# A graph layer with a routed feed-forward: a node group's step run whole after its own edges, and a shorter last group

## The chip, the cores and the metric

The kernel runs on one NeuronCore of one Trainium2 chip. The metric is device time in microseconds (us); lower is better. The engines are named as in the profile: PE (TensorE, matmuls; PEld its weight loads), DVE (VectorE), ACT (ScalarE), POOL (GpSimd), SP (SyncE, which here only issues DMAs).

## The reference

Twelve thousand five hundred nodes of 256 features go through a graph layer and a feed-forward layer that is routed to one of eight experts. Both are added to their input.

```python
# x (12500, 256); src, dst, edge_weight (212500,), dst sorted
msgs = _layernorm(x)[src] * edge_weight[:, None]
agg = segment_sum(msgs, dst, 12500)
x = x + agg @ W.T + b                          # W (256, 256)
xf = _layernorm(x)
H = gelu(xf @ W1 + b1)                         # W1 (256, 1024)
probs = softmax(H @ Wg + bg)                   # Wg (1024, 8)
e = argmax(probs)
x = x + probs[e] * (H @ Wd[e] + bd[e])         # Wd (8, 1024, 256)
```

## The kernel before

**Stages.** First the rows of `x` are normalized and written to a table in DRAM. Then comes the edge stage, which is most of the time: 212,500 edges in 1664 tiles of 128, sixteen tiles to a gather step (104 steps). Then the routed stage: 105 tiles of 128 nodes, sorted by expert, each gathered from `row_table`, multiplied with its expert's weights and scattered to the output.

**Edge stage, gather steps.** POOL issues one indirect DMA for each tile (L402), in order, into a ring of three sections of sixteen tiles. Ahead of every eighth tile it waits until PE has used up the tile that held the place (`s_edge_mm`, L401), so POOL can be at most 48 tiles ahead of PE. For a step PE multiplies the sixteen tiles with narrow one-hot weights into `psR` (L514; this is what frees the section), DVE copies the result to `parts` (L896), PE places the parts into the node columns (L523), and DVE adds them to the running sums `agg` (L886) and prepares the next step's weights (L843, L853).

**Edge stage, group steps.** Edges are sorted by destination, so after four or five gather steps all edges of a group of 512 nodes (four blocks of 128) are in. There are 25 groups (`NF`). A table of 129 steps, `steps_i`, worked out on the chip, tells PE and DVE at every turn of their loops whether a gather step or a group step is next. POOL reads no table and only gathers. A group step, f being the group whose edges are in, does two groups' work:

- for f, `take_sums` on DVE (L920: copy the sums out, clear them), `messages` on PE (L560: multiply with the graph weights), `normalize` on DVE (L993: residual, layer norm), `transpose_xn2` on PE (L570), and the copy `copy_xn2T` on ACT (L457);
- for f - 1, `rank_list` (PE), `hidden` on PE and ACT (the first feed-forward layer, eight chunks of two matmuls, a Gelu after each; then the gate matmul and 32 transposes), `rank_choices` and `add_to_lists` on DVE (they enter the choices of f - 2 into the expert lists), and `second_part` on DVE (copy the hidden rows out, choose the expert).

`messages` of f stands between the third and fourth chunk of `hidden` of f - 1. The first group's step is only its first half (kind `SECTIONS + 1`), and after the loop `hidden` of group 24 runs by itself. SP stores the two parts of the rows (`store_x2`, `store_rows`) and loads the next `x` in the same shifted order; the weights of the eight experts (8 MB) are loaded when the last sums are taken, behind `store_rows` of group 23 on SP. Group 24 holds 212 nodes, but all four blocks are computed and stored.

**End of the edge stage.** The last choices are entered in the lists, DVE builds the order of the nodes (up to L1089), and POOL begins the routed gathers (L416, L419).

Of the kernel before, what the change touches and what calls it, by code (L numbers as in the profile page):

```python
# [15 lines left out]
F32 = mybir.dt.float32  # L16
# [7 lines left out]
P = 128  # L24
N = 12500
# [11 lines left out]
NB = NODES // P  # L37
EDGES = 212500
# [30 lines left out]
PAD_ROW = N + (-N) % 64  # L69
# [23 lines left out]
def build(nc, x, srcT, dstT, wT, gnn_WT, gnn_b, W1, b1T, Wg, bg, Wd, bd, out):  # L93
    assert PAD_ROW + P <= NODES and NB % LN_ROWS == 0
    ctx = ExitStack()
    with ctx:
# [10 lines left out]
        row_dram = nc.dram_tensor("row_table", (NODES, ROW), F32, kind="Internal").ap()  # L107
# [28 lines left out]
        steps_i = sb("steps_i", [P, STEPS, 6], I32)  # L136
# [184 lines left out]
        def _(sp):  # L321
# [25 lines left out]
            def store_x2(f):  # L347

                sp.wait_ge(s_xn2, f + 1)
                sp.dma_start(row_dram[bass.ds(f * GROUP, GROUP), 0:C].rearrange("(q p) c -> p q c", p=P),  # L350
                             xg[:, :, :]).then_inc(s_x2_st, 16)
                sp.wait_ge(s_x2_st, f * 16 + 16)

            def load_x(f):
                sp.dma_start(xg[:, :, :], x[bass.ds(f * GROUP, GROUP), :]
                             .rearrange("(q p) c -> p q c", p=P)).then_inc(s_xg, 16)

            def store_rows(f):
                sp.wait_ge(s_rows, f + 1)
                sp.dma_start(row_dram[bass.ds(f * GROUP, GROUP), C:ROW].rearrange("(q p) c -> p q c", p=P),  # L360
                             rows[:, :, C:ROW]).then_inc(s_rows_st, 16)
# [19 lines left out]
            store_rows(NF - 1)  # L381
# [65 lines left out]
        def _(act):  # L447
# [9 lines left out]
            def copy_xn2T(f):  # L457
                for k in range(KC):
                    act.wait_ge(s_xt, f * KC + k + 1)
                    nc.scalar.activation(xn2T[:, k, :], psH[k][:, :], ACT.Identity).then_inc(s_xtc, 1)  # L460

            def hidden(f):
                for c in range(HC):
                    act.wait_ge(s_h, f * HC + c + 1)
                    nc.scalar.activation(hidT[:, c, :], psH[c % 2][:, :], ACT.Gelu,  # L465
                                         bias=b1[:, c:c + 1]).then_inc(s_gelu, 1)
                act.wait_ge(s_gp, f + 1)
                nc.scalar.activation(gate_parts[:, :], psG[:, :], ACT.Identity).then_inc(s_gc, 1)

            copy_xn2T(0)  # L470
# [23 lines left out]
        def _(pe):  # L494
# [44 lines left out]
            def rank_list(b):  # L539
# [4 lines left out]
                nc.tensor.matmul(psE[0][:, at], upper[:, :], oh, start=True, stop=False)  # L544
                for d in range(1, QB):
                    nc.tensor.matmul(psE[0][:, at.start + d * E:at.stop], ones[:, :], oh[:, 0:(QB - d) * E],
                                     start=False, stop=(d == QB - 1))
                for q in range(QB):
                    mm = nc.tensor.matmul(psE[0][:, total], ones[:, :], oh[:, q * E:(q + 1) * E],
                                          start=(q == 0), stop=(q == QB - 1))  # L550
                mm.then_inc(s_rank, 1)

            def extend_list(b):
                pe.wait_ge(s_rank_oh, b + 1)
                for q in range(QB):
                    mm = nc.tensor.matmul(psE[0][:, list_new], slot_oh[:, q, :], col_oh[:, q, :],  # L556
                                          start=(q == 0), stop=(q == QB - 1))
                mm.then_inc(s_list, 1)

            def messages(f):  # L560

                pe.wait_ge(s_aggs, f + 1)
                for q in range(QB):
# [4 lines left out]
                mm.then_inc(s_z, 1)  # L568

            def transpose_xn2(f):  # L570
                pe.wait_ge(s_xn2, f + 1)
                for k in range(KC):
                    for q in range(QB):
# [599 lines left out]
```

## Time and profile before

| | |
|---|---|
| median of 3 runs | 2784.89 us (2781.65 to 2785.08) |
| profiled execution | 2787.9 us, its span 2785.7 us |
| mean granted TensorE clock | 0.771 of full speed |
| busy | PE 66%, POOL 66%, PEld 44%, DVE 39%, ACT 16% |
| chain that ended last | POOL 57%, "issue" 20%, PE 20%, DVE 2%, DMA 1% |

No engine is near fully busy over the span, so the shares alone name no bound: the stages have to be read one by one. The chain that ended last is the work followed back from the last instruction, each piece to what released it. Its POOL part and most of its "issue" part (the issuing engine's own time between instructions) are the edge stage; its PE part is the end of the edge stage and the routed stage.

### The profile page before, as it was taken

The page shows a single profiled execution, that of the slowest core. Times are in us where ns is not written, and L with a number is a line of the kernel's source. Part 1 is how long each engine was busy: PE and PEld are TensorE (multiplying, and loading weights), DVE is VectorE, ACT ScalarE, POOL GpSimd, SP SyncE. Part 2 cuts the span into 40 slices and gives each one's busy share as a digit, 9 for nine tenths or more (in the row PEclk, how much of TensorE's full clock was granted, in tenths as well). Part 3 has the DMA queues.
Part 4 walks back from the last instruction along what each step waited for, and adds up shares of the span by engine and source line. Part 5 has one row for each costly group of instructions (what it writes and reads, how often), then busy time and mean ns, then how long its engine had stood idle before and what let it go on. Part 6 is the DMA issues. An engine that isn't in the chain of part 4 may idle for free.

```text
span 2785.7 us, 38476 instructions
## 1 busy us (share of the span) xinstructions
PE 1838.6 (66%) x10106; PEld 1214.5 (44%) x10107; DVE 1082.6 (39%) x3491; ACT 444.4 (16%) x847; POOL 1839.7 (66%) x1988
## 2 busy tenths in 40 slices
PE   0134675656756656666567566675666787999998
PEld 0022343433433334334334343343333446888887
DVE  8522443334433344333444334443334443333332
ACT  7000110101101001010011000110001123443332
POOL 0677777777777777777777777777777303555553
PEclk9955777767767677676777666776767788999999
DMA  9434444444444444444444344444444354555553
GB/s 395 150 103 118 150 149 118 134 149 147 149 119 133 150 148 148 120 136 146 150 149 148 112 141 147 151 147 118 133 149 149 96 200 149 183 183 180 182 179 127
DMA packets 153599, 420.31 MB, mean 151 GB/s; under 512 B 33321, under 2 KB 67500, under 8 KB 150881
## 3 DMA queue, kind: packets, MB, share of 16 engines
q0 software_dynamic: 100032, 300.27, 36.6%
q1 hardware_dynamic: 53536, 119.73, 11.7%
q14 instruction: 24, 0.19, 0.0%
q8 instruction: 7, 0.11, 0.0%
HBM read 328.02 MB, written 92.82 MB: 151 GB/s over the span
## 4 chain that ended last, share of the span: by engine, by line
POOL 57%; issue 20%; PE 20%; DVE 2%; DMA 1%; DVEq 0%; SPq 0%; POOLq 0%
POOL big L402 57%; PE psA L654 3%; PE psE L654 3%; PE psG L654 3%; PE psH L654 3%; PE psH L588 1%; DMA src_i<-in_srcT 1%; PE psH L644 1%; PE psA L644 1%; PE psE L644 1%; PE psG L644 0%; PE psR L644 0%; PE psA L610 0%; PE psG L596 0%; PE psR L514 0%
## 5 line engine op out<-in xcount | busy, mean ns | idle before, releaser
L402 POOL DMA_INDIRECT big<-xn_table,src_i x1664 | 1608.0, 966 | 581.5 <-issue 581.5
L514 PE MATMUL psR<-big,sel_narrow 128*32 128x256 f32 x3328 | 340.9, 580 | 509.2 <-DMA big<-xn_table,src_i 336.8
L514 PEld LDWEIGHTS psR<-big,sel_narrow 128*32 128x32 f32 x3328 | 139.1, 156 | 653.0 <-issue 545.4
L588 PE MATMUL psH<-xn2T,w 128*128 128x512 f32 x800 | 406.6, 667 | 0.0
L465 ACT ACTIVATE hidT<-psH,b 128x512 f32<-128x512 f32 x200 | 137.4, 687 | 1512.6 <-PE psH L588 1512.6
L523 PE MATMUL psE<-place,parts 128*128 128x80 f32 x832 | 173.3, 375 | 140.7 <-DVE parts L896 140.7
L588 PEld LDWEIGHTS psH<-xn2T,w 128*128 128x128 f32 x800 | 171.4, 218 | 202.0 <-issue 200.7
L523 PEld LDWEIGHTS psE<-place,parts 128*128 128x128 f32 x832 | 153.5, 276 | 221.1 <-DVE parts L896 221.1
L896 DVE COPY parts<-psR 128x512 f32<-128x512 f32 x104 | 71.7, 689 | 381.8 <-PE psR L514 381.8
L416 POOL COPY stage<-rel_f 128x1 int32 (+1 forms) x105 | 19.2, 183 | 223.3 <-DVEq L1094 116.5
L419 POOL DMA_INDIRECT rows<-row_table,stage x105 | 104.1, 991 | 86.8 <-POOL stage L416 86.8
L890 DVE TENSOR_TENSOR place<-iota,shift_f 128x160 f32<-128x160 f32 x104 | 33.8, 325 | 328.2 <-issue 328.2
L1021 DVE COPY rows<-psA 128x512 f32<-128x512 f32 x200 | 129.1, 686 | 40.5 <-PE psA L610 35.7
L427 POOL DMA_INDIRECT out<-big,st_out x105 | 107.3, 1022 | 43.6 <-issue 30.5
L610 PE MATMUL psA<-ident,hidT 128*128 128x128 f32 x800 | 123.4, 288 | 18.1 <-DVE rows L1021 17.7
L886 DVE TENSOR_TENSOR big<-psE,big 128x160 f32 x208 | 67.5, 325 | 156.0 <-PE psE L523 141.2
L610 PEld LDWEIGHTS psA<-ident,hidT 128*128 128x128 f32 x800 | 85.9, 143 | 87.7 <-DVE rows L1021 49.6
L999 DVE TENSOR_TENSOR big<-psA,big 128x512 f32<-128x512 f32 x50 | 32.2, 685 | 229.5 <-PE psA L565 229.5
L556 PE MATMUL psE<-col_oh,big 128*128 128x40 f32 x208 | 37.8, 343 | 96.1 <-DVE big L957 96.1
L654 PE MATMUL psA<-big,hidT 128*128 x432 | 98.9, 383 | 0.0
L565 PE MATMUL psA<-wt,aggs 128*128 128x256 f32 x400 | 93.4, 388 | 6.6 <-DVE aggs L926 6.6
L654 PE MATMUL psE<-big,hidT 128*128 x416 | 94.1, 379 | 0.0
(205 smaller groups left out, 2369.3 us busy)
## 6 DMA issues: line engine op xcount, KB each, us to landing
row_table<-rows SPq DMA_DIRECT2D x25, 2064.0 KB, 8.0
big<-xn_table,src_i POOLq DMA_INDIRECT x1664
big<-in_x SPq DMA_DIRECT2D x10, 1280.0 KB, 17.4
xn_table<-big SPq DMA_DIRECT2D x10, 1280.0 KB, 13.1
big<-in_x SPq DMA_DIRECT2D x25, 512.0 KB
row_table<-big SPq DMA_DIRECT2D x25, 512.0 KB, 3.9
big<-in_Wd SPq DMA_DIRECT2D x8, 1024.0 KB, 12.2
hidT<-in_dstT SPq DMA_DIRECT2D x2, 840.0 KB, 30.4
```

What stands on the lines that cost most here:

```text
L402: nc.gpsimd.indirect_dma_start(out=xring[:, h * STEP_TILES + j, :], out_offset=None, in_=xn_dram[:, :], in_offset=bass.IndirectOffsetOnAxi ...
L419: nc.gpsimd.indirect_dma_start(out=grow[i], out_offset=None, in_=row_dram[:, :], in_offset=bass.IndirectOffsetOnAxis(ap=st_in[:, i:i + 1], ...
L427: nc.gpsimd.indirect_dma_start(out=out[:, :], out_offset=bass.IndirectOffsetOnAxis(ap=st_out[:, i:i + 1], axis=0), in_=ybuf[i], in_offset= ...
L465: nc.scalar.activation(hidT[:, c, :], psH[c % 2][:, :], ACT.Gelu, bias=b1[:, c:c + 1]).then_inc(s_gelu, 1)
L514: mm = nc.tensor.matmul(psQ[j * LANES:(j + 1) * LANES, o * C:(o + 1) * C], sel_narrow[:, t, :], xring[:, t, :], start=(odd == 0), stop=(od ...
L523: mm = nc.tensor.matmul(psW[:, at:at + SPAN], parts[:, o, k * P:(k + 1) * P], place[:, o, :], start=True, stop=True)
L565: mm = nc.tensor.matmul(psA[q // 2][:, (q % 2) * C:(q % 2 + 1) * C], aggs[:, k, q * P:(q + 1) * P], wt[:, k, :], start=(k == 0), stop=(k = ...
L588: mm = nc.tensor.matmul(psH[c % 2][:, :], w1[:, k, c * P:(c + 1) * P], xn2T[:, k, :], start=(k == 0), stop=(k == KC - 1))
L610: mm = nc.tensor.transpose(psA[i % 2][:, j * P:(j + 1) * P], hidT[:, 4 * half + j, q * P:(q + 1) * P], ident[:, :])
L644: mm = nc.tensor.transpose(psT2[i][k][:, j * P:(j + 1) * P], grow[i][:, C + c * P:C + (c + 1) * P], ident[:, :])
L654: mm = nc.tensor.matmul(psY2[i], hT2[i][:, c, :], wd[:, bass.ds(e8 + c, 1), :], start=(c == 0), stop=(c == HC - 1))
L1021: nc.vector.tensor_copy(rows[:, q, C + half * 512:C + (half + 1) * 512], psA[i % 2][:, :]).then_inc(s_ev, 1)
```

## The change

Each group's step is now whole and in one place: `rank_list`, `messages`, `extend_list`, `transpose_xn2`, `hidden` for the same group f, all after f's edges are in. The first group's half step is gone, the loops have one branch less and the step table one kind and one field less (128 turns, the last group's step written behind the loop). The last group is computed and stored for two blocks. On SP the stores of a group follow one another, and the last group's two stores come behind the expert weights. Empty places in the routed tiles point to 32 pad rows instead of 128.

```diff
+LAST_QB = -(-(N - (NF - 1) * GROUP) // P)
-PAD_ROW = N + (-N) % 64
+PAD_LANES = 32
...
-            store_x2(0)
-            load_x(1)
             with sp.Fori(0, NF - 2) as f:
-                store_x2(f + 1)
-                load_x(f + 2)
+                store_x2(f)
+                load_x(f + 1)
                 store_rows(f)
-            store_x2(NF - 1)
+            store_x2(NF - 2)
+            load_x(NF - 1, LAST_QB)
             store_rows(NF - 2)
...
-            store_rows(NF - 1)
+            store_x2(NF - 1, LAST_QB)
+            store_rows(NF - 1, LAST_QB)
...
             with act.Fori(0, NF - 1) as f:
-                hidden(f)
-                copy_xn2T(f + 1)
-            hidden(NF - 1)
+                group_act(f)
+            group_act(NF - 1, LAST_QB)
...
+            def group(f, blocks=QB):
+                cols = blocks * P
+                rank_list(f)
                 pe.wait_ge(s_aggs, f + 1)
...
                 mm.then_inc(s_z, 1)
-            def transpose_xn2(f):
+                extend_list(f)
                 pe.wait_ge(s_xn2, f + 1)
...
-            def hidden(f, following=None):
-                rank_list(f)
                 pe.wait_ge(s_xtc, f * KC + KC)
                 for c in range(HC):
-                    if c == 3 and following is not None:
-                        messages(following)
...
-                extend_list(f)
                 pe.wait_ge(s_gelu, f * HC + HC)
...
-                if following is not None:
-                    pe.wait_ge(s_xn2, f + 2)
...
-            with pe.Fori(0, STEPS) as k:
+            with pe.Fori(0, STEPS - 1) as k:
...
                 with pe.If(kind == SECTIONS):
-                    before = n.with_bounds(min_val=0, max_val=NF - 2)
-                    hidden(before, before + 1)
-                    transpose_xn2(before + 1)
-                with pe.If(kind == SECTIONS + 1):
-                    messages(0)
-                    transpose_xn2(0)
-            hidden(NF - 1)
+                    group(n.with_bounds(min_val=0, max_val=NF - 2))
+            group(NF - 1, LAST_QB)
-            rank_list(NF)
-            extend_list(NF)
+            rank_list(NF, LAST_QB)
+            extend_list(NF, LAST_QB)
...
                     take_sums(link, f, g, slot, spill)
+                    rank_choices(tie, f)
                     normalize(link, f)
-                with dve.If(kind == SECTIONS):
-                    rank_choices(tie, before)
-                    add_to_lists(tie, before)
-                    second_part(tie, before)
+                    add_to_lists(tie, f)
+                    second_part(tie, f)
...
+            take_sums(link, last, NG, last % NS * SLOT, (last - 1) % NS * SLOT + GROUP, LAST_QB)
+            rank_choices(tie, last)
+            normalize(link, last, LAST_QB)
+            add_to_lists(tie, last)
+            second_part(tie, last, LAST_QB)
```

On PE, in the group step inside the loop, the first layer (`psH<-xn2T,w`, on the copied transposes `xn2T`) stood ahead of the messages (`psA<-wt,aggs`). Before:

```order
L549 MATMUL psE<-chosen,ones 128x8 x4
L588 MATMUL psH<-xn2T,w 128x512 [waits xn2T_copied]
L588 MATMUL psH<-xn2T,w 128x512 x3
L565 MATMUL psA<-wt,aggs 128x256 [waits aggs_ready]
L565 MATMUL psA<-wt,aggs 128x256 x7
L556 MATMUL psE<-col_oh,big 128x40 [waits list_onehots_ready]
L596 MATMUL psG<-hidT,wg 32x512 [waits gelu_done]
L617 MATMUL psE<-fold,big 128x8 x3
L574 MATMUL psH<-ident,big 128x128 [waits xn2_ready]
```

The same place of the changed kernel:

```order
L547 MATMUL psE<-chosen,ones 128x8 x4
L564 MATMUL psA<-wt,aggs 128x256 [waits aggs_ready]
L564 MATMUL psA<-wt,aggs 128x256 x7
L554 MATMUL psE<-col_oh,big 128x40 [waits list_onehots_ready]
L573 MATMUL psH<-ident,big 128x128 [waits xn2_ready]
L583 MATMUL psH<-xn2T,w 128x512 [waits xn2T_copied]
L583 MATMUL psH<-xn2T,w 128x512 x3
L590 MATMUL psG<-hidT,wg 32x512 [waits gelu_done]
L605 MATMUL psE<-fold,big 128x8 x3
```

The first layer has moved behind the transposes of its own group (`psH<-ident,big`), and those stand behind the wait for DVE's `xn2_ready`.

On SP, at the end of the edge stage, the last two stores were split by the expert weights. Before:

```order
L350 DMA row_table<-big 128x4x256 [waits xn2_ready]
L360 DMA row_table<-rows 128x4x1032 [waits rows_ready,x2_stored]
L378 DMA big<-in_Wd 128x8x256 [waits rows_stored,ffn_dve,edge_matmul_done]
L378 DMA big<-in_Wd 128x8x256 x7
L380 DMA big<-in_bd 128x2048
L360 DMA row_table<-rows 128x4x1032 [waits rows_ready]
```

Changed:

```order
L362 DMA row_table<-rows 128x4x1032 [waits rows_ready]
L378 DMA big<-in_Wd 128x8x256 [waits rows_stored,ffn_dve,edge_matmul_done]
L378 DMA big<-in_Wd 128x8x256 x7
L380 DMA big<-in_bd 128x2048
L354 DMA row_table<-big 128x2x256 [waits xn2_ready]
L362 DMA row_table<-rows 128x2x1032 [waits rows_ready,x2_stored]
```

Both stores of the last group now stand behind the weights, with two blocks each.

## Rows read from the trace of the kernel before

**Rows 1.** All gathers (L402): count, ns min/median/max, first and last start us.
```profile
L402 POOL DMA_INDIRECT big<-xn_table,src_i x1664: 942/946/1986, 76.9 to 2190.5; - x185
```

**Rows 2.** Chain that ended last, where it leaves POOL: start us, us, what.
```profile
2150.07 2.74 DMA big<-xn_table,src_i
```

**Rows 3.** Stretches in two group steps: us, engines' busy us, PEclk (granted clock), DMA.
```profile
1048.00:1051.00 3.00, 3.00 (x5) 1.45 (x6) 2.10 (x4) 0.00 (x0) 2.36 (x3) 0.50 0.34 94
1051.00:1068.00 17.00, 16.03 (x45) 8.22 (x44) 8.63 (x32) 5.50 (x8) 13.04 (x14) 0.99 0.36 102
2164.00:2171.00 7.00, 7.00 (x13) 3.47 (x14) 2.13 (x4) 0.69 (x1) 5.22 (x6) 0.52 0.36 98
2171.00:2186.00 15.00, 14.23 (x42) 7.48 (x40) 8.46 (x31) 4.82 (x7) 11.35 (x13) 1.00 0.37 104
```

**Rows 4.** Timeline of the first group's half step: start us, us, instruction, [idle before].
```profile
194.18 0.71 DVE L925 COPY aggs<-big 128x1024 f32 x1 [3.64 <-issue]
195.51 6.56 PE L565 MATMUL psA<-wt,aggs 128*128 128x256 f32 x16 [6.59 <-DVE aggs L926]
202.29 1.29 DVE L999 TENSOR_TENSOR big<-psA,big 128x512 f32<-128x512 f32 x2 [5.82 <-PE psA L565]
209.95 1.45 DVE L1010 TENSOR_SCALAR big<-big,meanvar,rstd 128x256 f32<-128x256 f32 x4
211.46 1.97 PE L574 MATMUL psH<-ident,big 128*128 128x128 f32 x8 [9.38 <-DVE big L1010]
213.47 0.60 ACT L460 ACTIVATE xn2T<-psH 128x512 f32<-128x512 f32 x1 [0.18 <-PE psH L574]
```

**Rows 5.** Timeline of a full group step in mid-stage.
```profile
1048.01 6.98 PE L588 MATMUL psH<-xn2T,w 128*128 128x512 f32 x12
1048.06 0.69 DVE L925 COPY aggs<-big 128x1024 f32 x1 [3.65 <-issue]
1058.28 8.75 PE L588 MATMUL psH<-xn2T,w 128*128 128x512 f32 x20
1083.36 0.19 DVE L989 TENSOR_TENSOR chosen<-route_b,valid 128x32 f32<-128x32 f32 x1
```

**Rows 6.** Timeline of the gather steps behind that group step.
```profile
1084.60 1.94 PE L514 MATMUL psR<-big,sel_narrow 128*32 128x256 f32 x32 [1.92 <-issue]
1092.68 0.71 DVE L853 TENSOR_TENSOR sel_narrow<-sel_narrow,w_f  x1
1108.72 0.68 DVE L853 TENSOR_TENSOR sel_narrow<-sel_narrow,w_f  x1
1121.39 0.69 DVE L896 COPY parts<-psR 128x512 f32<-128x512 f32 x1 [9.10 <-PE psR L514]
```

**Rows 7.** Gathers counted in 1033.8 to 1048 and in 1048 to 1095.2.
```profile
L402 POOL DMA_INDIRECT big<-xn_table,src_i x11: 942/946/1209, 1034.0 to 1046.8; - x11
...
L402 POOL DMA_INDIRECT big<-xn_table,src_i x38: 942/946/1510, 1048.0 to 1095.2; - x38
```

**Rows 8.** Timeline from the step of group 23's edges to the routed stage.
```profile
2164.26 0.71 DVE L925 COPY aggs<-big 128x1024 f32 x1 [3.63 <-issue]
2224.53 0.69 DVE L925 COPY aggs<-big 128x1024 f32 x1 [3.65 <-issue]
...
2265.35 17.88 SPq L378 DMA_DIRECT2D big<-in_Wd  x8
...
2277.53 0.69 ACT L465 ACTIVATE hidT<-psH,b 128x512 f32<-128x512 f32 x1 [1.03 <-PE psH L588]
2278.28 1.92 PE L596 MATMUL psG<-hidT,wg 128*32 128x512 f32 x16
2283.27 3.81 SPq L380 DMA_DIRECT2D big<-in_bd  x1
2288.48 0.19 DVE L989 TENSOR_TENSOR chosen<-route_b,valid 128x32 f32<-128x32 f32 x1
2307.45 0.22 DVE L1089 TENSOR_SCALAR rel_f<-xn2T 128x105 int32<-128x105 f32 x1
```

More of the change, by code:

```diff
@@ L93, in build @@
 def build(nc, x, srcT, dstT, wT, gnn_WT, gnn_b, W1, b1T, Wg, bg, Wd, bd, out):
-    assert PAD_ROW + P <= NODES and NB % LN_ROWS == 0
+    assert N + PAD_LANES <= ((NF - 1) * QB + LAST_QB) * P and NB % LN_ROWS == 0
     ctx = ExitStack()
@@ L537, in gather_step, with rank_list @@
                     pe.sem_inc(s_placed, 1)
-            def rank_list(b):
+            def rank_list(b, blocks=QB):
                 pe.wait_ge(s_chosen, b + 1)
@@ L568, in messages @@
                 mm.then_inc(s_z, 1)
-            def transpose_xn2(f):
+                extend_list(f)
                 pe.wait_ge(s_xn2, f + 1)
                 for k in range(KC):
-                    for q in range(QB):
+                    for q in range(blocks):
                         mm = nc.tensor.transpose(psH[k][:, q * P:(q + 1) * P],
@@ L595, in hidden @@
                     cg = c % 4
-                    mm = nc.tensor.matmul(psG[cg * GATE_COLS:(cg + 1) * GATE_COLS, :], wg[:, c, :], hidT[:, c, :],
-                                          start=(c < 4), stop=(c >= 4))
+                    mm = nc.tensor.matmul(psG[cg * GATE_COLS:(cg + 1) * GATE_COLS, 0:cols], wg[:, c, :],
+                                          hidT[:, c, 0:cols], start=(c < 4), stop=(c >= 4))
                 mm.then_inc(s_gp, 1)
-                if following is not None:
-                    pe.wait_ge(s_xn2, f + 2)
-                else:
-                    pe.wait_ge(s_ev, f * (2 * QB))
-                for i in range(2 * QB):
-                    half, q = i // QB, i % QB
+                for i in range(2 * blocks):
+                    half, q = i // blocks, i % blocks
                     if i >= 2:
@@ L614, in hidden @@
                 pe.wait_ge(s_listed, f + 1)
-                for q in range(QB):
+                for q in range(blocks):
                     mm = nc.tensor.matmul(psE[0][:, q * E:(q + 1) * E], gate_parts[:, q * P:(q + 1) * P],
@@ L918, in gather_step, with take_sums @@
                     narrow_weights(g + 1, start)
-            def take_sums(link, f, g, slot, spill):
+            def take_sums(link, f, g, slot, spill, blocks=QB):
                 dve.wait_ge(s_acc, g * STEP_TILES + ACC0)
@@ L924, in take_sums @@
                 here, before = agg[:, :, bass.ds(slot, GROUP)], agg[:, :, bass.ds(spill, P)]
-                link(nc.vector.tensor_copy(aggs[:, :, :], here))
+                link(nc.vector.tensor_copy(aggs[:, :, 0:blocks * P], here[:, :, 0:blocks * P]))
                 nc.vector.tensor_tensor(aggs[:, :, 0:P], aggs[:, :, 0:P], before, ALU.add).then_inc(s_aggs, 1)
@@ L931, in take_sums, with rank_choices @@
                                              None, ALU.add))
-            def rank_choices(tie, b):
+            def rank_choices(tie, b, blocks=QB):
                 dve.wait_ge(s_chosen, b + 1)
@@ L991, in choose, with normalize @@
+                nc.vector.tensor_tensor(chosen[:, 0:blocks, :], route_b[:, 0:blocks, :],
+                                        valid[:, bass.ds(f * QB, blocks)].unsqueeze(2).to_broadcast([P, blocks, E]),
                                         ALU.mult).then_inc(s_chosen, 1)
-            def normalize(link, f):
+            def normalize(link, f, blocks=QB):
                 dve.wait_ge(s_z, f + 1)
                 dve.wait_ge(s_xg, f * 16 + 16)
-                x2 = xg[:, :, :]
-                for a in range(2):
+                x2 = xg[:, 0:blocks, :]
+                for a in range(blocks // 2):
@@ L1012, in normalize, with second_part @@
                 o.then_inc(s_xn2, 1)
-            def second_part(tie, f):
+            def second_part(tie, f, blocks=QB):
                 dve.wait_ge(s_rows_free, f + 1)
                 dve.sem_inc(s_pass_dve, 1)
-                for i in range(2 * QB):
-                    half, q = i // QB, i % QB
+                for i in range(2 * blocks):
+                    half, q = i // blocks, i % blocks
                     dve.wait_ge(s_tr, f * (2 * QB) + i + 1)
```

168 lines of the change are left out of this document (79 added, 89 removed).

## The prediction

> **What bounds the kernel now.** I read the views in this order: the page's slices and chain, all gathers, the chain where it leaves POOL, the timeline of group steps, and the end of the edge stage. The gathers are the bound of the edge stage. There are 1664, and from the first to the last start they take 2113.6 us, 1.271 us each [rows 1]. A gather lasts 0.946 us and the next follows 0.30 us later throughout, so POOL never waits for a free section. A gather step of sixteen tiles therefore costs POOL 20.3 us, a round of four steps 81.3 and one of five 101.7, whatever PE and DVE do meanwhile. The chain stays on POOL until the gather issued at 2150.07 [rows 2]. From there on PE and DVE set the end: group 23's step, two gather steps, group 24's step, and 83 us from the last `take_sums` until the node order stands [rows 8]. In mid-stage PE and DVE wait for data: the fourth gather step behind a group step finds its tiles 9.1 us late [rows 6]. So the edge stage has a cover of some us for each round, and the uncovered part is its end. The change spends the first and shortens the second, and the sum is a difference of two terms of like size.
>
> **A group's step, inside the loop.** I count from the start of `take_sums` to the end of `chosen`. Before, that is 35.5 us in the step at 1048.06 [rows 5]. The new order has no row of its own in full, but the first group's half step is its first half exactly: copy sums, messages, normalize, transposes, copies, with nothing beside them [rows 4].
>
> - Sums to messages: 195.51 less 194.18, 1.3 us. `rank_list` ends earlier and hides behind it.
> - Messages: 6.56 us at the low clock [rows 4]. In the full steps the granted clock is at half (1.2 GHz) when matmuls begin and full (2.4 GHz) from about 3 us on in one step and about 6 us in another [rows 3]; with 4.5 us for the middle, the rest of the messages takes half, and they end at 6.9 us (6.3 to 7.9).
> - Normalize: 202.29 to 211.40 [rows 4], 9.1 us, and 0.2 us to get there: 16.2. `rank_choices` now lies ahead of it on DVE; at 3 us it fits beside the messages. `extend_list` fits into PE's wait.
> - Transposes and ACT copies: 211.46 to 214.07, 2.6 us [rows 4], and 0.1: 18.9.
> - First layer: 15.7 us where the clock rose after 3 us [rows 5], about 17 where after 6; PE has idled 8 us before, so I take the middle, 16.3: 35.2. ACT's second table load hides behind the first chunk.
> - Last Gelu to gate 0.75 us, gate to the end of `chosen` 10.4 us in the last step of before, where the gate ran at the full clock [rows 8]. There DVE was adding to the lists at first; without that, 10.0.
>
> The sum is 46.0 us (45.2 to 47.2), about 10 more than before.
>
> **A round.** Behind the group, three gather steps that find their data take from 1083.55 to 1109.40, 25.9 us [rows 5, 6]. A fourth without waiting isn't in the trace; the second and third take 8.0 on average, so 8.0 (7.3 to 8.5). From the last weights to `take_sums` is 3.65 us of table loads and branches [rows 5]. The loops lose a branch, and this wait half a load; no row shows these alone, so between 0 and 1.2 us a round, and I take 0.6. Together 46.0 + 25.9 + 8.0 + 3.65 - 0.6 = 82.9 us against POOL's 81.3. The cover of a four-step round is used up and 1.6 us are over. There are 18 such rounds ahead of group 23's step: 29 us (0 to 63, from the ends of both ranges).
>
> **The ring.** A five-step round has 20 us more of cover on PE's side, but POOL's lead ends it. At `take_sums` POOL has issued 11 gathers beyond the step just used up; 37 of the 48 places remain, and the 38th gather starts 47.1 us later [rows 7]. It may only start when the next step's matmuls are through. Before, that was 38.5 us after `take_sums` (1086.54, [rows 6]). Now it is 46.0 + 1.9 (PE comes off the group a microsecond sooner, since the transposes are gone) = 47.9, so POOL waits 0.8 us. Five such rounds: 4 us (0 to 10). In four-step rounds the 0.8 lies within the 1.6. The waits for `s_edge_mm` in POOL's queue hold back only further gathers.
>
> **The end.** From `take_sums` of group 23 to the node order: before 2307.67 - 2164.26 = 143.4 us [rows 8]. After: 46.0 for group 23's own step; two gather steps, 9.8 and 8.0 less 0.3, 17.5; behind the loop no table loads, 0.3; the step of group 24 with two blocks; then the lists. The step with two blocks: `rank_list` comes late here, so messages end at 5.2 (half of 6.6, from 1.9 on); normalize 6.4 and 0.25 (its four wide operations, 1.3 to 1.45 us each, halve; its thirteen short ones stay); transposes and copies 1.8; first layer 9.1 (half of 13.7 to 17, and the slow stretch weighs more); Gelu, gate, four row copies instead of eight and choice 6.8. That is 29.6 (27 to 33). From `chosen` to the node order 19.0 before [rows 8], two less with half the list matmuls and one-hots: 17.0. Sum 110.4, a gain of 33 us (29 to 36).
>
> **SP and the rest.** The expert weights start when the last sums are cleared, as before, and take 21.7 us to issue [rows 8]; the routed stage starts 46 us after `take_sums` now, against 43 us from their start before, so they aren't later than needed. The last group's stores stand behind them: `x2` from about 24 us on, both landed some 4 us ahead of the routed gathers. If that cover fails, a few us. The routed stage has the same 105 tiles. Smaller stores, the shorter table and 32 pad rows cost nothing in an uncovered place.
>
> **Sum.** 29 + 4 - 33 = 0 on the profiled execution's 2787.9 us, and so on the median, 2784.9, which is 3 lower. Short steps can't give back what long ones cost, and a shorter fourth step would; I leave both out but for 2 us towards the shorter step, the nearest rows being its neighbours at the high clock: 2783 us.
>
> **The rivals.** *The cover holds* (faster): if the step is 45.0 us or less, or the fourth gather step is nearer 7, a round stays within 81.3 us, POOL never stops and the end's gain is all: about 2752 us. For it: the clock may rise early in both dense stretches. Against it: this needs more than 1 us of 46.
>
> *The cover is gone* (slower): if messages and first layer both meet the late clock rise, the step is 47.5 us; every us counts in 23 rounds, so 1.5 us more cost 34: about 2818 us. It decides from a step of some 46.3 us on. For it: PE idles 8 us in every step ahead of the first layer, and 6 us of half clock do stand in the rows [rows 3]. Against it: on the average of many steps the rise came between.
>
> *The first layer never gets the full clock*: 32 matmuls of 0.85 us (twice the 0.44 of 8.75 us for 20, [rows 5]) are 27.4 us, the step 57 us, the rounds 11 us longer each, the time about 3045 us. The rows speak against it: the layer's matmuls alone brought the clock from 0.52 to 1.00 in a step that had begun cold [rows 3]. The Trainium skill ("TensorE: Matmul & The Clock Gate", "HAM oscillation — how this bites in real kernels") says that matmul stages cut by waits are throttled again at every wait, which speaks against this change; by the trace that holds at the wait, but not for the whole of a 16 us layer.
>
> *It doesn't overlap less*: that PE would still run another group's layer meanwhile is excluded by its fixed order; 1 in 100.
>
> **How the numbers follow.** The forecast, within some 12 us of 2783, 0.45; the cover holds 0.20; the cover is gone 0.30; the clock stays low 0.04; the rest 0.01. A measurement of this kernel can tell about 0.2%, 5.6 us, from no change. Of the forecast's 0.45, 0.18 lie below that, 0.20 within it, 0.07 above. With the rivals: faster 0.38, same 0.22, slower 0.40 (some of each rival lies near the middle, too). The range leaves out the low clock and the outer parts of both other rivals: 2750 to 2820. The forecast's own range is 2771 to 2795.
>
> **What would show it.** In the profile after: `take_sums` to `chosen` of 46 us in the loop, rounds of four steps at about 83 us instead of 81.3; the fourth gather step no longer waiting for its tiles; gaps of about a us ahead of a gather on POOL, once a round; the last gather some 30 us later than 2190.5; `take_sums` of the last group to the node order 47 us instead of 83. A last gather still at 2190 would show the cover held; gaps of 3 us or more on POOL that it was gone; first-layer matmuls at 0.85 us throughout the clock rival. The prediction is wrong, too, if POOL's pace itself changes, or if the routed stage waits for the last stores.

## The result and the profile after

The changed kernel takes 2796.65 us (median of 5 runs, 2794.17 to 2799.62), the kernel before 2783.45 in the same set (2781.65 to 2785.08). The ratio is 1.0045, with a 95% interval of 1.0033 to 1.0056: slower by almost half a per cent, where the forecast was 2783 and no change. The profiled execution took 2794.17 us; its span of 2792.2 is 6.5 more than before. The medians lie further apart than the spans: the profiled execution of before was 4 us above the median of its set, that of after 2 below. The sums below are made on spans and explain these 6.5 us. What the medians lie apart beyond that is not shown: only the profiled execution of each set has a trace.

The chain that ended last, from the page of after (shares of the span by engine):

```profile
PE 53%; POOL 13%; DVE 13%; issue 12%; DVEq 4%; DMA 3%; ACT 1%; SPq 0%; POOLq 0%
```

POOL had 57% of that chain before, PE 20%. The chain of after now runs through the group steps most of the time.

The gathers, as a group of the page (busy us, mean ns of one; then POOL's idle time ahead of them and what ended it). Before:

```profile
L402 POOL DMA_INDIRECT big<-xn_table,src_i x1664 | 1608.0, 966 | 581.5 <-issue 581.5
```

After (the line is L403 here):

```profile
L403 POOL DMA_INDIRECT big<-xn_table,src_i x1664 | 1620.2, 974 | 609.7 <-issue 575.6 <-PE psR L511 34.1
```

All gathers of after: count, ns min/median/max, first and last start, and who waited for them:

```profile
L403 POOL DMA_INDIRECT big<-xn_table,src_i x1664: 940/947/1999, 76.9 to 2230.9; - x185
its engine sat idle before it (us, times) until:
  issue: 575.6, 1642
  PE psR L511: 34.1, 22
```

The last gather starts 40.4 us later than in [rows 1], and these lines say from what: 28.2 us more idle time, since POOL now waits 22 times for PE to free a section, and 12.2 us more busy time, since the gathers themselves got longer. The first part was forecast, the second was not. This says how POOL spent the 40.4 us, not yet what made them; the second profile below tells.

A group's step, from the timeline of after (as in [rows 4, 5]):

```profile
1063.49 0.76 DVE L902 COPY aggs<-big 128x1024 f32 x1 [3.08 <-issue]
1064.87 5.12 PE L564 MATMUL psA<-wt,aggs 128*128 128x256 f32 x16 [0.97 <-DVE aggs L903]
1070.13 1.29 DVE L976 TENSOR_TENSOR big<-psA,big 128x512 f32<-128x512 f32 x2 [1.10 <-PE psA L564]
1077.80 1.45 DVE L987 TENSOR_SCALAR big<-big,meanvar,rstd 128x256 f32<-128x256 f32 x4
1079.30 1.97 PE L573 MATMUL psH<-ident,big 128*128 128x128 f32 x8 [8.49 <-DVE big L987]
1081.95 15.40 PE L583 MATMUL psH<-xn2T,w 128*128 128x512 f32 x32 [0.69 <-ACT xn2T L461]
1098.13 1.92 PE L590 MATMUL psG<-hidT,wg 128*32 128x512 f32 x16 [0.78 <-ACT hidT L465]
1107.96 0.19 DVE L966 TENSOR_TENSOR chosen<-route_b,valid 128x32 f32<-128x32 f32 x1
```

That is 44.7 us here; the 24 steps of the loop lie between 44.6 and 47.0, 45.9 on average. Messages take 5.1 to 6.7 and the first layer 15.4 to 16.2. Behind it, in the same round:

```profile
1108.72 3.58 PE L511 MATMUL psR<-big,sel_narrow 128*32 128x256 f32 x32 [2.38 <-issue]
1112.61 0.94 POOL L403 DMA_INDIRECT big<-xn_table,src_i  x1 [1.57 <-PE psR L511]
1113.81 0.68 DVE L820 TENSOR_TENSOR sel_narrow<-iota,rel_f 128x512 f32 x1
1113.87 1.45 POOL L403 DMA_INDIRECT big<-xn_table,src_i  x1 [0.31 <-issue]
1135.52 3.64 PE L511 MATMUL psR<-big,sel_narrow 128*32 128x256 f32 x32 [4.25 <-DMA big<-xn_table,src_i]
```

The second line is the ring's wait: POOL stands still until PE's first gather step behind the group is through, 49 us after `take_sums`. The last line shows POOL's wait coming back to PE: the fourth gather step finds its tiles late. The two lines between them show a gather that takes longer, of which more below.

The first `take_sums` of after, and the end of its edge stage (as in [rows 4] and [rows 8]):

```profile
193.68 0.75 DVE L902 COPY aggs<-big 128x1024 f32 x1 [3.09 <-issue]
...
2203.96 0.74 DVE L902 COPY aggs<-big 128x1024 f32 x1 [3.10 <-issue]
2268.55 0.43 DVE L902 COPY aggs<-big 128x512 f32<-128x512 f32 x1
2270.45 17.97 SPq L378 DMA_DIRECT2D big<-in_Wd  x8
2297.52 0.17 DVE L966 TENSOR_TENSOR chosen<-route_b,valid 128x16 f32<-128x16 f32 x1
2302.02 0.38 SPq L362 DMA_DIRECT2D row_table<-rows  x1
2314.55 0.22 DVE L1069 TENSOR_SCALAR rel_f<-xn2T 128x105 int32<-128x105 f32 x1
```

From the first `take_sums` to that of group 23, 18 rounds of four steps and 5 of five, after takes 2010.3 us where before took 1970.1 (2164.26 less 194.18). A four-step round takes 83.1 us on average, 81.1 before, and a five-step round 102.7, 101.9 before. So the four-step rounds lose 36 us and the five-step rounds 4.

From `take_sums` of group 23 to the node order it takes 110.8 us, against 143.4 before. The order stands 7.1 us later all the same, since it started 39.7 us later. The routed stage takes 477.4 us behind it, 478.0 before.

### The profile page after: what moved, and what is told of

Read it like the earlier page. It is cut to its first block, busy times and chain, and to the rows that moved or that the text cites. A ratio compares the mean times of both kernels' runs of the same rounds, so it can differ in the third digit from the quotient of the medians.

```text
span 2792.2 us, 37965 instructions
## 1 busy us (share of the span) xinstructions
PE 1853.9 (66%) x10062; PEld 1245.6 (45%) x10063; DVE 1077.6 (39%) x3477; ACT 475.7 (17%) x871; POOL 1852.4 (66%) x1988
## 4 chain that ended last, share of the span: by engine, by line
PE 53%; POOL 13%; DVE 13%; issue 12%; DVEq 4%; DMA 3%; ACT 1%; SPq 0%; POOLq 0%
PE psH L583 14%; POOL big L403 13%; PE psR L511 7%; PE psA L564 5%; PE psA L636 3%; PE psH L636 3%; PE psG L636 3%; PE psE L636 3%; PE psE L520 3%; PE psA L598 3%; DVEq L309 2%; DVE rows L998 2%; PE psH L573 2%; PE psG L590 2%; DMA big<-xn_table,src_i 2%
## 5 line engine op out<-in xcount | busy, mean ns | idle before, releaser
L403 POOL DMA_INDIRECT big<-xn_table,src_i x1664 | 1620.2, 974 | 609.7 <-issue 575.6
L511 PE MATMUL psR<-big,sel_narrow 128*32 128x256 f32 x3328 | 352.5, 597 | 354.4 <-DMA big<-xn_table,src_i 152.3
L583 PE MATMUL psH<-xn2T,w 128*128 128x512 f32 (+1 forms) x800 | 387.8, 648 | 17.0 <-ACT xn2T L461 17.0
L461 ACT ACTIVATE xn2T<-psH 128x512 f32<-128x512 f32 (+1 forms) x50 | 29.4, 588 | 1676.3 <-PE psH L573 1676.3
L520 PE MATMUL psE<-place,parts 128*128 128x80 f32 x832 | 164.6, 361 | 144.2 <-DVE parts L873 144.2
L573 PE MATMUL psH<-ident,big 128*128 128x128 f32 x196 | 48.4, 428 | 210.0 <-DVE big L987 210.0
L465 ACT ACTIVATE hidT<-psH,b 128x512 f32<-128x512 f32 (+1 forms) x200 | 135.9, 679 | 239.9 <-PE psH L583 239.9
L564 PE MATMUL psA<-wt,aggs 128*128 128x256 f32 x392 | 145.4, 550 | 14.7 <-DVE aggs L903 14.6
L417 POOL COPY stage<-rel_f 128x1 int32 (+1 forms) x105 | 19.3, 184 | 189.0 <-DVEq L1102 105.7
L573 PEld LDWEIGHTS psH<-ident,big 128*128 128x128 f32 x196 | 38.4, 223 | 213.0 <-DVE big L987 213.0
L564 PEld LDWEIGHTS psA<-wt,aggs 128*128 128x128 f32 x392 | 111.1, 291 | 40.9 <-DVE aggs L903 16.7
## 6 DMA issues: line engine op xcount, KB each, us to landing
big<-in_Wd SPq DMA_DIRECT2D x8, 1024.0 KB, 11.9
```

The source lines that it names most:

```text
L403: nc.gpsimd.indirect_dma_start(out=xring[:, h * STEP_TILES + j, :], out_offset=None, in_=xn_dram[:, :], in_offset=bass.IndirectOffsetOnAxi ...
L465: nc.scalar.activation(hidT[:, c, 0:blocks * P], psH[c % 2][:, 0:blocks * P], ACT.Gelu, bias=b1[:, c:c + 1]).then_inc(s_gelu, 1)
L511: mm = nc.tensor.matmul(psQ[j * LANES:(j + 1) * LANES, o * C:(o + 1) * C], sel_narrow[:, t, :], xring[:, t, :], start=(odd == 0), stop=(od ...
L520: mm = nc.tensor.matmul(psW[:, at:at + SPAN], parts[:, o, k * P:(k + 1) * P], place[:, o, :], start=True, stop=True)
L564: mm = nc.tensor.matmul(psA[q // 2][:, (q % 2) * C:(q % 2 + 1) * C], aggs[:, k, q * P:(q + 1) * P], wt[:, k, :], start=(k == 0), stop=(k = ...
L573: mm = nc.tensor.transpose(psH[k][:, q * P:(q + 1) * P], xn2[:, q, k * P:(k + 1) * P], ident[:, :])
```

## The experiments

The theory after the result: the shorter end gives back what was forecast; the loop loses because a four-step round no longer fits into POOL's pace, and perhaps because gathers take longer. Rivals in turn: the loss is the ring's alone, the chain of a round's alone, or chance of one profile. The kernel before ran in each set; its medians there were 2783.45 (with the result), 2785.57 (`ring4`, `ring4_before`, `warm`, `half_release`), 2785.71 (`warm8`, `warm8_half`, `full_last`, `extra_add`) and 2787.65 (`after_again`, `short_only` and the two runs at the end). All ratios are to the kernel before in the same set.

**A second profile, `after_again`.** No edit.

> The changed kernel unaltered, for a second profiled execution. In the first the last gather started 40.4 us later than in the kernel before: 27.9 us of waiting ahead of gathers, 0.2 of it elsewhere, and 11 us because gathers themselves took longer (43.2 us in all above 0.96 each, against 33.1). If both parts belong to the kernel, the second profile shows 25 to 36 us of waiting and 38 to 46 above 0.96 us, and the time is 2793 to 2800. If the longer gathers were chance of one execution, they are back near 33 here.

Measured: 2797.93 us (2789.93 to 2801.98), ratio 1.0036 (1.0023 to 1.0048). Its gathers:

```profile
L403 POOL DMA_INDIRECT big<-xn_table,src_i x1664 | 1614.5, 970 | 614.8 <-issue 575.2
L403 POOL DMA_INDIRECT big<-xn_table,src_i x1664: 940/946/1977, 77.1 to 2230.4; - x185
```

The idle part is 33.3 us above before and the busy part 6.5. So the waiting is a property of the kernel, 28 to 33 us. The gathers are longer again, but by another amount, and the last one starts where it did: 2230.4 instead of 2230.9, though the gathers took 5.7 us less. POOL waited 5.1 us more instead. The 23 rounds take 2010.9 us, within a us of the first profile. So here the rounds of PE and DVE and the ring set when POOL can go on, and a longer gather mostly takes the place of a wait; that it costs the changed kernel time of its own is not shown.

**Each half of the change alone.** `full_last` has whole steps and four blocks in the last group:

```
-LAST_QB = -(-(N - (NF - 1) * GROUP) // P)
+LAST_QB = QB
```

> The changed kernel with its last group computed, stored and entered for four blocks as in the kernel before: the other part of the change alone (the whole step, not the two blocks). All theories: the last step takes 46.5 to 47 us instead of 29.1 and the lists 2 us more, 19 to 20 us in all, nothing else: 2814 to 2818. If the two larger stores behind the expert weights land late, some us more.

Measured: 2815.97 us, ratio 1.0104 (1.0087 to 1.0121). The last group's step and the node order in it:

```profile
2270.73 0.69 DVE L902 COPY aggs<-big 128x1024 f32<-128x1024 f32 x1
2317.01 0.19 DVE L966 TENSOR_TENSOR chosen<-route_b,valid 128x32 f32<-128x32 f32 x1
2336.27 0.22 DVE L1069 TENSOR_SCALAR rel_f<-xn2T 128x105 int32<-128x105 f32 x1
```

The step is 46.5 us instead of 29.1, and the lists take 19.3 instead of 17.1. The loop loses what it lost in the changed kernel (the last gather starts 43.1 us later than before), and the end is still 15 us shorter than before (128.5). `short_only` is the other half: the kernel before, overlap kept, with two blocks in the last group.

```
...
-            hidden(NF - 1)
-            rank_list(NF)
+            hidden(NF - 2, NF - 1, next_blocks=LAST_QB)
+            transpose_xn2(NF - 1, LAST_QB)
+            hidden(NF - 1, blocks=LAST_QB)
+            rank_list(NF, LAST_QB)
...
```

> The kernel before, its overlapped group steps kept, with only the last group cut to two blocks (and the last turn written behind the loop): the other half of the change alone. Theory: POOL never waits, as before, so the edge stage stays; the end gets shorter by half of group 24's first layer, its gate and copies of the rows (11 us) and by the lists (2 us): 2770 to 2776 where the kernel before has 2784 to 2786. If the last group's half were hidden behind other work the time would be that of before.

Measured: 2769.72 us, ratio 0.9936 (0.9923 to 0.9949), 0.3 us below the expected range. POOL never waits:

```profile
L406 POOL DMA_INDIRECT big<-xn_table,src_i x1664 | 1605.7, 965 | 581.6 <-issue 581.3
```

So the two blocks alone gain 18 us, and whole steps alone cost 30; together that is 12, and the whole change cost 13 and 10 in its two sets. The last group's half was worth having, and the kernel with overlap can have it too.

**Is it the ring or the chain? `ring4`.** Four sections of sixteen tiles; the room comes from the running sums.

```
-SECTIONS = 3
+SECTIONS = 4
...
-NS = 1 << (2 + -(-STEP_TILES * P // GROUP) - 1).bit_length()
+NS = 4
...
```

> The changed kernel with four ring sections (64 tiles) instead of three; the space comes from the running sums, which keep four group slots instead of eight. Theory A (no room to be late): without waiting, PE and DVE need about 83.1 us for a four-step round and 91 for a five-step round, 1951 us for the 23 rounds against POOL's 1970, so they are fast enough on average and lose only because a ring of 48 tiles lets no round be late. With 64 tiles a round may be 20 us late: POOL's gaps after a group step go, the last gather starts at about 2192 instead of 2230.9, and the time falls to 2750 to 2765 us. Theory B (the chain of the four-step rounds is the bound): the ring is not what is short; only the five-step rounds give back their 4 us, the last gather stays after 2220, the time 2785 to 2795.

Measured: 2769.71 us, ratio 0.9942 (0.9929 to 0.9955): between the two theories. POOL's waiting is gone and the last gather starts at 2195.0, as theory A had it:

```profile
L406 POOL DMA_INDIRECT big<-xn_table,src_i x1664 | 1612.6, 969 | 581.4 <-issue 580.5
```

But A's sum of an unhindered chain was too low. With the tiles there in time, a four-step round still took 84.4 us on PE and DVE (mean of 18) and a five-step round 93.8, 1989 us in all, where the rounds of the kernel before, at POOL's pace, took 1970. `take_sums` of group 23 comes at 2182.2, 18 us later than in [rows 8]. The fourth gather step without any late tile, from the timeline:

```profile
2168.77 0.68 DVE L833 TENSOR_TENSOR sel_narrow<-sel_narrow,w_f  x1
2171.06 3.64 PE L514 MATMUL psR<-big,sel_narrow 128*32 128x256 f32 x32 [3.24 <-issue]
```

The weights are there at 2169.45 and PE starts 1.6 us later, for no wait that the profile shows; what it does meanwhile stays open. So of the 40 us that the rounds lost, the longer ring gives back 21, and 19 are the chain's. The ring decides what a late round does to POOL, and the chain how late rounds are: both are needed for the loss. The control, `ring4_before`, has the same edit in the kernel before:

> Control: the kernel before with the same fourth section. Its POOL waited for no free section (gap 0.30 us throughout), so both theories give no change: 2783 us, within 6. A gain of 10 us or more would say that the longer ring, or the smaller sums, help by something else, and would take that much from the run ring4.

Measured: 2789.53 us, ratio 1.0014 (1.0005 to 1.0023). The fourth section by itself gains nothing.

**A little slack in the ring, `half_release`.**

```
-                    mm.then_inc(s_edge_mm, STEP_TILES)
+                        mm.then_inc(s_edge_mm, OCT)
```

> The changed kernel with PE reporting a gather step's tiles as used up after the first eight and again after the second eight, instead of all sixteen at its end: POOL's first wait behind a group step ends 0.9 us (full clock) to 1.7 us (low clock) sooner. A: that is 0.9 to 1.7 us of lateness allowed, which removes the stall of most rounds with a 45 us step (0.8 to 1.3 us each) but not that of rounds with a 47 us step (84.2 us on PE and DVE): 10 to 20 us less, 2777 to 2787. B: the chain of the rounds is unchanged, so no change: 2792 to 2798.

Measured: 2777.11 us, ratio 0.9965 (0.9952 to 0.9978), at the lower end of theory A's range. POOL's waits:

```profile
POOL big L403 <- PE psR L511: 21.1, 21, 2.7
```

They fell from 34.1 to 21.1 us. One line in the changed kernel turns its loss into a small gain.

**The length of the step.** Three runs change it. `extra_add` makes it 1.25 us longer on DVE:

```
...
+                link(nc.vector.tensor_tensor(xn2[:, 0:blocks, :], x2,
+                                             gnn_b_bc[:, :].unsqueeze(1).to_broadcast([P, blocks, C]), ALU.add))
                 link(nc.vector.tensor_tensor(x2, x2, gnn_b_bc[:, :].unsqueeze(1).to_broadcast([P, blocks, C]), ALU.add))
```

> The changed kernel with the wide addition of the bias done twice in normalize (the first into a tensor that is overwritten): 1.25 us more in each group's step. A2: every us counts in all 23 rounds and in the last two steps, 24 to 25 times 1.25 with half of it in the last group: 28 to 32 us more, 2825 to 2829. B2, the step's length matters little: under 10 us more, below 2807.

Measured: 2826.56 us, ratio 1.0149 (1.0131 to 1.0167), 30 more than the changed kernel. POOL's waits:

```profile
POOL big L403 <- PE psR L511: 69.6, 30, 5.1
```

That is twice the 34.1. The step grew to 47.7 us, 1.8 more: beside the 1.25 us of the addition, the first layer took 16.3 us on average instead of 15.8. So each us of step cost POOL 20 us of waiting and the kernel 17. The gathers' busy time was 1615.3 us, 4.9 less than in the changed kernel, and the time rose all the same. `warm` and `warm8` shorten it, with matmuls of constants in PE's wait for the normalized rows:

```
                 extend_list(f)
+                for _ in range(WARM * blocks // QB):
+                    nc.tensor.matmul(psG[:, :], w1[:, 0, 0:P], w1[:, 1, 0:512], start=True, stop=True)
```

With WARM = 12:

> The changed kernel with twelve extra matmuls of constants (128x512, result unused; six in the last group) on PE while it waits for the normalized rows, so that the clock does not fall. A: the first layer then runs at the full clock, 13.8 us instead of 15.4 to 16.1, and the gather steps behind it too; the group step falls from 45.9 us to 44.0 or less, a four-step round to POOL's 81, and the time to 2755 to 2770. B: the same step, but if the fourth gather step still ends late the round stays above 82 and the time at 2780 or more. Rival C, that the extra matmuls end after the normalized rows are ready: the step stays at 45 to 47 and the time at 2790 to 2800.

Measured: 2767.04 us, ratio 0.9931 (0.9919 to 0.9944). A step of `warm`:

```profile
1165.25 10.55 PE L571 MATMUL psG<-w 128*128 128x512 f32 x24
1172.42 1.45 DVE L990 TENSOR_SCALAR big<-big,meanvar,rstd 128x256 f32<-128x256 f32 x4
1175.63 1.04 PE L576 MATMUL psH<-ident,big 128*128 128x128 f32 x8
1177.41 14.00 PE L586 MATMUL psH<-xn2T,w 128*128 128x512 f32 x32 [0.74 <-ACT xn2T L462]
```

The first layer takes 14.00 us instead of 15.4 to 16.2, and the transposes 1.04 instead of 1.97. But the transposes start 1.76 us after the rows are ready (1173.87): the filling was too long, and the step is 45.2 us in nearly every group, as the rival C had it. The time is in A's range none the less: no step is at 47 us any more, and the fourth gather step takes 7.8 us instead of 9.1, so that a four-step round takes 82.0. With WARM = 8:

> The run warm with eight extra matmuls (four in the last group) instead of twelve. With twelve they ended 1.75 us after the normalized rows were ready, and the step took 45.2 us in every group, though the first layer fell to 14.0. Theory A2 (what decides is the length of the group's step against what POOL's pace and the ring allow, about 44 us): with eight the step is 43.5 us, a four-step round is POOL's 80.3 to 81.3, POOL's gaps behind group steps vanish, the last gather starts before 2200 and the time is 2748 to 2757. Theory B2 (the gather steps behind the group are the bound, the step's length matters little): the rounds stay at 81.8 as in warm, the time at 2763 to 2768. If the clock falls again in the us between the extra matmuls and the transposes, the first layer is back at 15.4 and the step at 44.5 or more: 2765 to 2780.

Measured: 2763.06 us, ratio 0.9927 (0.9911 to 0.9943). The step is 43.9 us on average, and POOL almost never waits, but the time is 6 above A2's range and just inside that of B2, and the last gather starts at 2206.2, not before 2200. Its gathers say why:

```profile
L404 POOL DMA_INDIRECT big<-xn_table,src_i x1664 | 1620.9, 974 | 584.3 <-issue 579.6
```

The idle part is back near 581, the busy part is still 12.9 us above before. The last gather starts 15.7 us later than in [rows 1], the 12.9 and 2.8 us more of waiting. A four-step round takes 81.6 us, near the 81.8 of B2; but if the gather steps on PE and DVE were the bound, as B2 has it, POOL would have to wait for them. Both together, `warm8_half`:

> warm8 and half_release together. A2: if warm8 alone frees POOL, this adds nothing beyond 3 us; where warm8 leaves gaps on POOL, this takes them, and the time is 2745 to 2755. B2: 2755 to 2765.

Measured: 2760.82 us, ratio 0.9916 (0.9901 to 0.9931), the fastest here, below both kernels, but again in B2's range (2755 to 2765) and above A2's:

```profile
L404 POOL DMA_INDIRECT big<-xn_table,src_i x1664 | 1616.1, 971 | 581.5 <-issue 579.7
```

No waiting is left, and 8 us of longer gathers are; the last gather starts 8.1 us later than in [rows 1], at 2198.6.

**Why do gathers get longer?** In the timeline of after, DVE and POOL side by side:

```profile
1070.45 0.94 POOL L403 DMA_INDIRECT big<-xn_table,src_i  x1 [0.30 <-issue]
1071.45 1.22 DVE L980 TENSOR_TENSOR big<-big,gnn_b_bc 128x1024 f32<-128x1024 f32 x1
1071.69 1.80 POOL L403 DMA_INDIRECT big<-xn_table,src_i  x1 [0.30 <-issue]
1073.80 0.94 POOL L403 DMA_INDIRECT big<-xn_table,src_i  x1 [0.30 <-issue]
```

The gather that starts inside the addition ends at 1073.49, 0.82 us after the addition. So does the one at 1113.87 further up: DVE's L820 ends at 1114.49, the gather at 1115.32. In the whole trace of before, 121 gathers take over 0.98 us; 112 of them start inside L853, L1003, L843, L890 or the copy at L925, and all of these end 0.81 to 0.84 us after that DVE operation. (Five start while L928 clears the sums, four in the setup ahead of the first step.) A gather that is already running when one of the five operations begins is not held in this trace (0.945 us on average). Nor are those that start inside L1010, which has one tensor operand, or, in after, inside L976, which reads one of its two from PSUM, where matmuls write: 0.946 us. The other traces have one exception, the copy of the sums:

```profile
720.04 1.18 POOL L403 DMA_INDIRECT big<-xn_table,src_i  x1 [0.31 <-issue]
720.42 0.69 DVE L902 COPY aggs<-big 128x1024 f32 x1 [3.06 <-issue]
```

This is `extra_add`. The gather was running for 0.37 us when the copy began, and ends 0.12 us after the copy. Over all the traces, 38 gathers that had begun 0.25 to 0.50 us ahead of this copy did so; those that had begun up to 0.12 us, or 0.53 us and more, ahead of it were not held.

The Trainium skill ("SBUF — State Buffer", "SBUF: two separate sides") says that VectorE and GpSimd share a pair of ports as an exclusive lock, which a VectorE operation with two inputs in SBUF can hold against a GpSimd instruction that reads SBUF, and that an fp32 copy within SBUF keeps GpSimd from writing the descriptors of its DMAs. These rows agree: a gather, which reads its indices `src_i` from SBUF, is held to the end of such an operation when it starts inside it, and then needs 0.82 us more. The same section reports a probe in which `tensor_tensor` did not stall a DMA; here it delays gathers.

Two runs on the kernel before, where POOL sets the pace, tried this on the time. `before_two_adds` has the edit of `extra_add`:

> The kernel before with the wide addition of the bias done twice in normalize (first into a tensor that is overwritten). POOL sets the pace here and has 9 us of cover in a round, so 1.25 us more on DVE is covered by itself. Theory P (a gather that starts beside a wide DVE operation with two operands in SBUF is held until that ends): 25 more such operations, in each group's step, lengthen the gathers by 8 to 17 us in all, the last gather starts that much later, and the time is 2793 to 2805. Rival Q (gathers are long for reasons of their own, as transfers or their queue): the last gather stays within 3 us, the time 2784 to 2788.

Measured: 2806.22 us, ratio 1.0067 (1.0054 to 1.008), with no waiting on POOL:

```profile
L402 POOL DMA_INDIRECT big<-xn_table,src_i x1664 | 1622.3, 975 | 581.5 <-issue 581.5
```

The gathers are 14.3 us longer in sum and the last starts 14.4 us later, the size that theory P had; the time is a us above P's range, since the end, from group 23's sums to the node order, takes 3.1 us more as well. But P's reason is not what the trace shows. The gathers that start inside the two additions take 6.8 us over 0.946 us each in sum, those inside the single one of before 8.8: the second addition holds next to nothing (0.2), since it mostly begins while a gather held by the first is still running. The growth is beside other operations, above all the copy at L925 (from 1.0 to 10.8 us) and L843 (from 7.6 to 11.9), which DVE now reaches at another time. `before_no_add` takes the addition away:

```
...
-                link(nc.vector.tensor_tensor(x2, x2, gnn_b_bc[:, :].unsqueeze(1).to_broadcast([P, QB, C]), ALU.add))
```

It leaves the bias out of the result.

> The kernel before without that addition (the bias is left out of the result). Theory P: the 8.4 us by which gathers beside it were longer are gone, the last gather starts 6 to 9 us sooner, the time 2774 to 2780. Rival Q: within 3 us of the kernel before.

Measured: 2785.82 us, ratio 0.9993 (0.9984 to 1.0001), no gain and inside the rival Q's range, and the gathers did not get shorter:

```profile
L402 POOL DMA_INDIRECT big<-xn_table,src_i x1664 | 1616.5, 971 | 581.8 <-issue 581.8
```

Neither theory had 8.5 us more. (The last gather starts 8.9 us later; the end, 6.0 us shorter, about makes up for it.) By DVE operation, what the gathers beside it took above 0.946 us: the 8.8 us beside the addition are gone, but the weights' multiplication (L853) went from 13.3 to 24.2 and the copy at L925 from 1.0 to 7.2. So one operation more and one less both made the sum longer, by shifting what DVE does afterwards against POOL's gathers. That gathers are held is shown row by row; what sum a given timing makes was not worked out.

The sum also moves without any such edit. Three kernels with DVE's order of before have 1605.7 (`short_only`), 1608.0 and 1613.0 us of gathers (`ring4_before`), the changed kernel 1620.2 and 1614.5, and `full_last`, with the same loop, 1614.6. So the new order does make gathers longer, by 7.5 us on these averages, with a scatter nearly as large.

## Why the prediction was wrong

**The end** was right: 110.4 forecast, 110.8 measured, a gain of 32.6 for 33. The last step took 29.1 us for 29.6, and from `chosen` to the node order 17.1 for 17.0. The expert weights and both stores of the last group were no hindrance.

**The group's step** was right: 46.0 forecast, 45.9 measured, with the first layer at 15.4 to 16.2 for 16.3 and the messages' end at 6.5 to 8.0 for 6.9. The clock rose in each layer (0.86 to 0.91 granted over the layer), so the rival of a low clock is out; the runs with filled waits show that its fall in the wait costs about 1.4 to 2.2 us of first layer and 0.9 of transposes.

**The round** is the step that failed, by its size: its 29 us for the four-step rounds measured 36. The mechanism was right, a round that no longer fits into POOL's pace and a ring that stops POOL. The sum took 82.9 us against 81.3, 1.6 us over; measured were 83.1 against 81.1, 2.0 us over, 18 times. On the side of PE and DVE, errors of opposite sign met, and that was luck: the fourth step took 9.1 us rather than 8.0, and `ring4`, with the same 9.1 and no late tiles, shows that it does not take late tiles for this; the three steps before it took 25.2 rather than 25.9, and the group's step in these rounds 45.8. On POOL's side, the pace of 1.271 us a gather gives 81.3 us, but the four-step rounds of before took 81.1 on average. The ring's 4 us for the five-step rounds measured 4.1; PE left the first gather step behind a group 48.5 us after `take_sums` on average, not 47.9, since in rounds such as the one shown its matmuls take 3.6 us at a granted clock of 0.51.

So the sum 29 + 4 - 33 came out as 36 + 4 - 33: the node order stands 7.1 us later, and the span is 6.5 longer. The medians lie 13 and 10 us apart in the two sets; the rest of that has no trace and stays open. A smaller misreading did not enter the sum: the 9.1 us in [rows 6] are DVE's idle time and contain PE's own matmuls, 3.6 us. In the rounds of before the fourth step took 14.7 us on average, against 9.1 without late tiles, so the cover was 5.6 us.

**POOL's pace** was wrong as a statement, too. A gather step costs POOL 20.3 us "whatever PE and DVE do meanwhile", says the first paragraph of the prediction. That was read from a mean and a median, and the spread between them was taken as fixed. A mean of 966 ns over a median of 946 is 33 us of longer gathers in sum, and DVE makes them. The change reorders DVE's whole step, and those 33 became 45 in the first profile and 40 in the second. The term was zero in the sum, and measured 12.2 and 6.5 us. In the changed kernel it is not what made the miss, since POOL's waits shrank and grew against it (28.2 and 33.3 us, the rounds 2010.3 and 2010.9). Where POOL does not wait it counts in full, as in `warm8_half`.

**The sign.** The 2 us towards a shorter fourth step pointed the wrong way: the neighbours at the high clock were not its like. The rival "the cover is gone" was given the right place, and its trigger, a step of 46.3 us, was met in about half of the steps (46.4 to 47.0), the others lying at 44.6 to 45.2. Its slope was steep: 23 us per us of step forecast, 17 measured in `extra_add`. The rival "the cover holds" is what `warm8` and `warm8_half` became, at 2763 and 2761 instead of 2752, and the difference is mostly the longer gathers. The range, 2750 to 2820, held the time; the narrow range of the forecast, 2771 to 2795, did not.

## What to carry to other kernels

A queue that never waits is not thereby independent: compare the mean of its instructions with their median, find what stands beside the long ones, and give that sum a term when the change moves it and the queue sets the pace. Where the queue waits for something else, ask first whether the wait takes the longer instructions up, as here. A difference of two large terms needs both sides of each term from rows of the same kind: here 0.4 us on a round of 81, 18 times, was the miss. When overlap is spent from a cover, the cover is the smaller of two things, the slack of the chain and the room in the ring between producer and consumer; here each us of step beyond it cost 17 us. When a change has two halves, cost and try them apart: one half here was worth 18 us and the other cost 30.

## What the runs showed of the hardware

A POOL gather that starts while DVE runs certain operations on SBUF ends 0.81 to 0.84 us after that operation (112 of 112 in the trace of before), instead of 0.946 us after its own start. Ones already running were seen held by the copy of the sums alone, when they had begun 0.25 to 0.50 us ahead of it (38 in all the traces); they ended 0.12 us after the copy. Twelve otherwise useless matmuls in PE's wait brought the layer behind them from 15.4 to 16.2 us down to 14.0 in every step, at a granted clock of 1.00; eight (7.1 us in an 8.5 us wait) did so in 16 of 24 steps, with 15.7 us in the others, and brought the time of the changed kernel from 2797 to 2763. In `ring4` PE needed 1.6 us to begin a gather step for which everything was ready, with no wait in the profile.
